# Layer 3 of a four-layer graph network: per-slot maxima on VectorE, and the destinations' scores brought to slots and edges one group earlier

## The reference

```python
h = (x @ W).reshape(N, 4, 32)
a_src = jnp.sum(h * att_src, axis=-1)        # 4 numbers a node
a_dst = jnp.sum(h * att_dst, axis=-1)
logits = leaky_relu(a_src[src] + a_dst[dst], 0.2)
seg_max = segment_max(logits, dst)
e = jnp.exp(logits - seg_max[dst])
denom = segment_sum(e, dst)
out = segment_sum(h[src] * (e / (denom[dst] + 1e-16))[:, :, None], dst)
```

## Time and profile before

| | us |
|---|---|
| median of three runs | 6190.91 |
| span of the profiled execution | 6206.6 |
| first gather of layer 3 starts | 3844.5 |
| last gather of layer 3 starts | 6151.8 |
| POOL busy, idle in that stretch | 1533.8, 786.1 |

### The profile page before, as it was taken

How to read it: one execution, slowest core, us unless ns; L and a number is a source line. 1 busy time by engine, 2 the same in 40 slices (tenths; PEclk the granted TensorE clock), 3 DMA queues, 4 the chain that set the end, 5 groups by cost and what they waited for, 6 DMA issues and landing times.

```text
span 6206.6 us, 70880 instructions
## 1 busy us (share of the span) xinstructions
PE 4537.9 (73%) x24017; PEld 3664.7 (59%) x24017; DVE 2510.7 (40%) x8563; ACT 1744.9 (28%) x3903; POOL 3119.8 (50%) x3324
## 2 busy tenths in 40 slices
PE   6999978988898988888898997254454444554445
PEld 5888865666666666666668997244343444443444
DVE  8999953333333333333335443123232222223224
ACT  5888842222222222222224553001110111101111
POOL 0000036666666666666650002666666666666664
PEclk9999989999999999999999998566566666666657
DMA  6777766655555565555556785222222222222221
GB/s 152 165 166 166 165 162 181 182 175 179 178 179 177 180 180 175 181 179 177 179 158 185 242 244 161 47 48 49 48 49 49 50 49 49 50 48 49 49 48 36
DMA packets 472459, 804.76 MB, mean 130 GB/s; under 512 B 72607, under 2 KB 301130, under 8 KB 462122
## 3 DMA queue, kind: packets, MB, share of 16 engines
q0 software_dynamic: 140192, 443.73, 28.7%
q1 hardware_dynamic: 317802, 346.76, 18.4%
q10 hardware_dynamic: 14112, 9.74, 0.5%
HBM read 663.72 MB, written 136.22 MB: 129 GB/s over the span
## 4 chain that ended last, share of the span: by engine, by line
PE 46%; another core or an unknown queue 29%; DVE 13%; issue 8%; DMA 1%; ACT 1%; POOL 0%; DVEq 0%; ACTq 0%
PE bank L1027 13%; PE bank L1014 11%; PE bank L1198 7%; PE bank L682 5%; DVE ring L1336 3%; PE bank L662 3%; DVE ring L980 2%; DMA atab<-at 1%; PE bank L1549 1%; PE bank L583 1%; DVE hs L631 1%; DVE tops L1286 1%; DVE hs L629 1%; DVE top L1290 1%
## 5 line engine op out<-in xcount | busy, mean ns | idle before, releaser
L543 POOL DMA_INDIRECT ring<-ptab,src x1612 | 1525.4, 946 | 850.4 <-issue 444.7
L543 POOL DMA_INDIRECT ring<-htab,src x1612 | 1533.8, 952 | 786.1 <-issue 465.7
L1027 PE MATMUL bank<-ring,oh 128*126 128x384 f32 x3224 | 1263.9, 508 | 32.2 <-issue 31.4
L980 DVE TENSOR_TENSOR ring<-bank,ring 128x512 f32<-128x512 f32 x806 | 543.6, 688 | 1609.3 <-PE bank L1014 737.1
L1549 PE MATMUL bank<-ring,oh 128*126 128x132 f32 x3224 | 714.5, 355 | 615.8 <-issue 605.6
L1014 PE MATMUL bank<-w1e,ea 128*128 128x256 f32 x3224 | 897.0, 401 | 244.1 <-DVE ring L980 161.1
L1549 PEld LDWEIGHTS bank<-ring,oh 128*126 128x126 f32 x3224 | 612.3, 255 | 706.9 <-issue 696.6
L1014 PEld LDWEIGHTS bank<-w1e,ea 128*128 128x128 f32 x3224 | 623.9, 200 | 528.4 <-issue 286.4
L996 ACT ACTIVATE ring<-ring 128x1024 f32<-128x1024 f32 x403 | 425.6, 1056 | 1364.8 <-DVE ring L980 1040.8
L1027 PEld LDWEIGHTS bank<-ring,oh 128*126 128x126 f32 x3224 | 625.9, 197 | 297.3 <-issue 83.5
L682 PE MATMUL bank<-xhl,at 128*126 128x258 f32 x3822 | 713.2, 323 | 0.0
(11 more groups left out here) (271 smaller groups left out, 4600.7 us busy)
## 6 DMA issues: line engine op xcount, KB each, us to landing
atab<-at POOLq DMA_DIRECT2D x78, 1543.5 KB, 9.9
ring<-ea_r SPq DMA_DIRECT2D x403, 256.0 KB
ea<-ea_t SPq DMA_DIRECT2D x403, 256.0 KB
adjb<-atab SPq DMA_DIRECT2D x156, 535.5 KB, 4.6
adjb<-atab SPq DMA_DIRECT2D x78, 472.5 KB, 4.4
ring<-ptab,src POOLq DMA_INDIRECT x1612
ring<-htab,src POOLq DMA_INDIRECT x1612
ptab<-pO ACTq DMA_DIRECT2D x49, 128.0 KB, 7.3
```

The lines of the kernel that those rows point to most:

```text
L543: return e.indirect_dma_start(o, None, table, bass.IndirectOffsetOnAxis(ap=src[:, t:t + 1], axis=0))
L980: e.tensor_tensor(group1(gi, m % 2), MLP[m % 3][:, :].rearrange("p (g f) -> p g f", g=2), group1(gi, m % 2), ALU.add).then_inc(s_edge, 1)
L1027: w = e.matmul(SUM[s % 2][0:SL, 0:384], slots_of(s, i), rv1[:, t // G % NR1, t % G, :], start=i == 0, stop=t == END[s])
```

## The change

The group's path is re-dealt. Offsets become d = u-1, a = u-2, g = u-3, c = u-4.

- **Group u**, which is just being gathered: DVE (k = 1) makes `hots` and `oh2`, k = 3 `away` (0 or -BIG, edge x slot, now from `hots` on DVE). PE (k = 4) transposes `hots` and `oh2`, both as real transposes; ACT (k = 8) copies out `ohT` and `o2T` alone. None of this needs gathered rows.
- **Group d = u-1**: PE (k = 2) brings `a_dst` to the slots into bank 5 (`s_dst`); DVE (k = 6) keeps it (`dsts`) and makes `wide4`; PE (k = 11) brings it to the edges with `ohT` (`s_ad`, half as many columns as before); ACT (k = 14) copies it into `edges`.
- **Group a = u-2**: DVE waits for the landing (before, ACT did, for u-1), adds `away` to the gathered `a_src` for each slot (`mask`, 504 columns), turns it in 32x32 squares, takes the maximum over 32, folds the four partition quarters by copies and maxima at offsets 64 and 32, spreads the result back over the quarters, picks each slot's own number with `quad` (`top`), turns the maxima back over all edges, multiplies by `hots` and adds up, so each edge has its slot's maximum without TensorE. Then logits from `edges`, `Exp` on ACT (k = 16), and the three weighings at k = 18, 19, 20.
- **Sums** of g = u-3 start at k = 0 (before, k = 4). The matmuls against `sel`, the transposing of `pk`, and the copies `pk`, `rT`, `away` on ACT are gone, `sel`'s making too. `mB` and `rB` share the memory of `held`.

```diff
-            L3A, L3B, L3G, L3C = 1, 2, 3, 4
-            LAG3 = 4
+            L3D, L3A, L3G, L3C = 1, 2, 3, 4
...
+            def before3(e, p, k):
+                if k == 1:
+                    if p >= NH:
+                        e.wait_ge(s_turn, p - NH + 1)
+                    e.tensor_tensor(hots[:, p % NH, :, :], ...
+                    if p >= ND:
+                        e.wait_ge(s_add3, p - ND + 1)
...
+                elif k == 3:
+                    e.tensor_scalar(away[:, p % NH, :, :], hots[:, p % NH, :, :], 1.0, BIG, ALU.subtract, ALU.mult).then_inc(
+            def dst3(e, d, k):
+                if k == 6:
+                    e.wait_ge(s_dst, d + 1)
+                    if d:
+                        e.wait_ge(s_ad, d)
+                    e.tensor_copy(dsts[0:SL, d % 4, :], dst_slots(d)).then_inc(s_wide, 1)
+                    e.tensor_tensor(wide4[0:SL, :, :], mine[0:SL, :].unsqueeze(2).broadcast_to([SL, GT, 4]),
...
+            def most3(e, a, k):
+                n = SIZE[a]
+                if k == 0:
+                    e.wait_ge(s_away, a + 1)
+                    e.wait_ge(*landed3(a))
+                    e.tensor_tensor(by_tile(mask, n), rows3(a, 0, n)[:, :, 128:132]...
+                elif k == 1:
+                    e.transpose(turned[:, :, :], back).then_inc(s_peak, 1)
+                elif k == 2:
+                    e.tensor_reduce(peak[:, :], turned[:, :, :], AX.X, ALU.max).then_inc(s_peak, 1)
+                elif k == 3:
+                    e.tensor_copy(other[0:64, :], peak[64:128, :]).then_inc(s_peak, 1)
+                elif k == 4:
+                    e.tensor_tensor(half[0:64, :], peak[0:64, :], other[0:64, :], ALU.max).then_inc(s_peak, 1)
...
+            def logits3(e, a, k):
+                if k == 9:
+                    e.transpose(back, peaks[:, :].unsqueeze(2).broadcast_to([P, 16, 32])).then_inc(s_pick, 1)
+                elif k == 10:
+                    e.tensor_tensor(tb, tb, each_head(hots[:, a % NH, :, :], n), ALU.mult).then_inc(s_pick, 1)
+                elif k == 11:
+                    e.tensor_reduce(zt[:, 1, 0:n, :].rearrange("p t h -> p h t"), tb, AX.X, ALU.add).then_inc(s_pick, 1)
+                elif k == 12:
+                    e.wait_ge(s_edges, a + 1)
...
             def tensor3(e):
-                        if 0 <= a < NS and k == 4:
-                            e.wait_ge(s_pack, a + 1)
-                            e.transpose(bank[4][0:4 * n, P:2 * P], pk[:, 0:n, :].rearrange("p i h -> p (i h)"), ident[:, :])
...
-                            for h in range(4):
-                                e.matmul(bank[5][0:SL, h * P:(h + 1) * P], sel[0:4 * n, h, :], rT[0:4 * n, :], start=True, stop=True)
...
+                        if u < NS and k == 4:
+                            e.wait_ge(s_hot, 2 * u + 2)
...
+                        if 0 <= d < NS and k == 2:
+                            e.wait_ge(s_copied, d + 1)
...
+                        if 0 <= d < NS and k == 11:
+                            e.wait_ge(s_wide, 2 * d + 2)
...
-                        g, i = divmod(GT * (u - L3G) + k - LAG3, GT)
+                        if 0 <= g < NS and k < SIZE[g]:
+                            if k % CH == 0:
+                                e.wait_ge(s_weigh, chunk(g, k))
```

More of the change, by code:

```diff
@@ L167, in build @@
         oh2f = oh2[:, :, :].bitcast(F32)
-        sel = sb("sel", [G * GT, 4, SL])
         mine = sb("mine", [P, GT])
@@ L1221, in expected @@
             N3 = -(-(max(POST3) + 1) // GT)
-            s_pack, s_hot, s_turn, s_away, s_copied, s_spread, s_tops, s_top, s_lim, s_wide, s_logit_in, s_logit, s_exp, s_weigh = (
-                sem(f"s_{n}") for n in ("pack", "hot", "turn", "away", "copied", "spread", "tops", "top", "lim", "wide", "logit_in",
-                                        "logit", "exp", "weigh"))
-            s_acc3 = sem("s_acc3")
+            s_hot, s_away, s_turn, s_copied, s_dst, s_wide, s_ad, s_mask, s_peak, s_top, s_lim, s_pick, s_logit, s_exp, s_weigh = (
+                sem(f"s_{n}") for n in ("hot", "away", "turn", "copied", "dst", "wide", "ad", "mask", "peak", "top", "lim",
+                                        "pick", "logit", "exp", "weigh"))
+            s_acc3, s_quad, s_edges = (sem(f"s_{n}") for n in ("acc3", "quad", "edges"))
             def odd_from(s):
@@ L1439, in vector3 @@
                 e.wait_ge(s_clear2, 1)
+                e.memset(mask[:, :, :], 0.0)
+                e.memset(quad[:, :], 0.0).then_inc(s_mask, 1)
+                e.wait_ge(s_mask, 1)
+                for k in range(4):
+                    m = e.memset(quad[32 * k:32 * k + 32, k:k + 1], 1.0)
+                m.then_inc(s_quad, 1)
+                e.wait_ge(s_quad, 1)
                 for u in range(N3):
-                    a, b, g = u - L3A, u - L3B, u - L3G
+                    d, a = u - L3D, u - L3A
@@ L1455, in scalar3 @@
                     for k in range(GT):
[L1456 to L1472 removed]
+                        if u < NS and k == 8:
+                            nb = B1[u] - B0[u] + 1
+                            e.wait_ge(s_turn, u + 1)
+                            if u >= 2:
+                                e.wait_ge(s_ad, u - 1)
+                            e.activation(ohT[0:SL, u % 2, :], bank[4][0:SL, 0:P], ACT.Copy)
+                            if u:
+                                e.wait_ge(s_dst, u)
@@ new lines, in tensor3 @@
+                        if 0 <= d < NS and k == 2:
+                            e.wait_ge(s_copied, d + 1)
+                            if d:
+                                e.wait_ge(s_wide, 2 * d)
+                            for i in range(B0[d], B1[d] + 1):
+                                m = e.matmul(dst_slots(d), o2T[:, i - B0[d], :], hs[:, i, 132:136], start=i == B0[d],
+                                             stop=i == B1[d])
+                            m.then_inc(s_dst, 1)
+                        if 0 <= d < NS and k == 11:
+                            e.wait_ge(s_wide, 2 * d + 2)
+                            if d:
+                                e.wait_ge(s_edges, d)
+                            e.matmul(bank[7][:, 0:4 * GT], ohT[0:SL, d % 2, :],
+                                     wide4[0:SL, :, :].rearrange("p t h -> p (t h)"), start=True, stop=True).then_inc(s_ad, 1)
```

274 lines of the change are left out of this document (137 added, 137 removed).

## The result

The changed kernel takes **6199.3 us** (median of 20 runs, 6192.1 to 6207.0); beside it, the kernel before took 6190.4 us (20 runs, 6183.1 to 6201.5). The ratio is 1.0016, with a 95% interval of 1.0010 to 1.0022: 9 to 10 us slower, real but within the 0.2% that I had called the same. The forecast of 6157 us was wrong. What came is rival 2's outcome, though not for rival 2's reason.

The account below looks back on a forecast made before the run. Layer 3 was taken as bound by POOL, stopped once a group by held TensorE answers. Terms -46 - 12 + 20 + 4 = -34 us took the 6206.6 us span to 6173, with the span 15.7 above the median 6157 us; range 5990 to 6330.

Parts of the forecast that it names:

- rival 2: Nothing comes of it: stop length independent of the number of answers, first stop's gain lost to longer gathers; 6180 to 6200; chance 0.17.
- the - 46 us for fewer TensorE instructions: POOL's stop in layer 3: 22 fewer TensorE instructions at 0.028 us shorten it 0.6 us a group, 77 groups.
- the + 4 us for the tail: From last gather to end, 53 us: one more DVE-heavy unit replaces one with two TensorE answers; ends 0 to +10.
- What bounds the kernel: Layer 3: POOL bound, stopped about 3.7 us a group because TensorE's answers are held while it gathers; cycle 30.0 us.
- Longer gathers (+ 20 us): POOL's gathers in layer 3: DVE's new SBUF-only operands lengthen them by 0.25 us a group.
- rival 4: DVE blocks POOL: each two-input or copying SBUF instruction holds a gather for its own length; +170 us, 6310; chance 0.08.
- The first stop (- 12 us): POOL's first stop in layer 3, 16.4 us after 105 gathers, shortens as group 0's sums need fewer answers; ends 0 and -16.
- VectorE's 4.5 us a group: DVE's net added work per group, covered by its wait for `tops`: 0 on the path, 347 us without that cover.
- Two answers in series, `dst` within the grace: TensorE's `s_dst`, then `s_ad`: `dst` by about 4 us, within some 6 us of grace; one stop a group as now.
- Rival 3: A second late TensorE answer: `dst` misses the grace, two stops a group, +285 us, 6460; in a third, 6270; chance 0.21.
- The signs that I had named: Changed profile: 78 waits of about 3.4 us, gather median 944 ns, first stop under 8 us, DVE about 13 us a group.
- The sentence on what would make the forecast wrong: Prediction wrong if DVE's own chain, not TensorE's answers, sets the unit, or held answers don't depend on POOL's gathering.

Follow-up runs that it names:

- e17: Kernel before, layer 3's gathers fetching 64 rows instead of 128, on a chip with stops: 6196.2 us, ratio 1.0011.
- e10: Kernel before with two one-column fillings on POOL behind each gather of layer 3: 6191.3 us, ratio 1.0005.
- e15: Kernel before with a 200-column filling on POOL behind each gather of layer 3, on a chip with stops: 6186.9 us, ratio 0.9998.
- e1: Changed kernel whose summing matmuls in layer 3 read only the upper 16 bits, 42 recorded instructions a group for 84: 6184.2 us, ratio 0.9992.
- e4: Changed kernel with 22 more transposes (44 recorded TensorE instructions) a group: 6209.0 us, ratio 1.0032.
- e9: Changed kernel, unchanged, run again beside the kernel before on a chip with stops: 6199.5 us, ratio 1.0020.
- e2: Kernel before with 4.5 us more VectorE work a group, six chained additions of 512 columns from SBUF: 6202.3 us, ratio 1.0023.
- e3: Changed kernel with a ring of four groups of gathered rows instead of five: 6189.7 us, ratio 0.9998.
- e11: Changed kernel with a ring of three groups of gathered rows instead of five: 6177.5 us, ratio 0.9981.
- e16: Changed kernel with a ring of three groups instead of five, second run: 6170.4 us, ratio 0.9968.
- e18: Changed kernel with a ring of three groups instead of five, third run: 6170.6 us, ratio 0.9966.
- e14: Changed kernel, unchanged, on a chip without stops: 5561.3 us against 5566.7 for the kernel before, ratio 0.9990.
- e12: Kernel before with a ring of three groups instead of five, on a chip with stops: 6509.8 us, ratio 1.0524.
- e5: Kernel before, unchanged, traced again on another chip, one without stops: 5569.0 us.
- e13: Kernel before with a 200-column filling on POOL behind each gather of layer 3, on a chip without stops: 5786.3 us against 5566.7, ratio 1.0394.

## Why the prediction was wrong, step by step

Two terms of the sum failed: the - 46 us for fewer TensorE instructions, which the runs put at 7, and the + 4 us for the tail, which measured + 22 to + 27. Under the first lies the cause that I had given to the stop.

**What bounds the kernel.** "POOL, with a stop once a group" was the right view on the wrong cause. On these chips POOL's mean pace in layer 3 is not set by its own work or by the kernel's other loads tried here. Three kernels whose POOL would by itself take 1.21 (e17), 1.26 (e10) and 1.40 us a gather (e15) had their gathers 1.421, 1.430 and 1.425 us apart. A stop has no length of its own; it is the rest, and grows with the gathers since the last one: 21 x (1.43 - 1.26) = 3.6 us, the 3.7 that I read from the earlier trace rows. "Held answers" are what this looks like from the other engines.

**The 0.028 us an instruction (- 46 us), the term that failed.** I read it from a short group: 18 tiles, stop 3.69 us instead of 3.99 and 4.06. Three tiles fewer are 12 TensorE instructions fewer, and also three gathers fewer; the second is what counts, 3 x 0.17 = 0.5 us. One row can't tell two quantities apart that always go together. e1 and e4 moved them apart and gave 0.004 us, 7 us for the 22 instructions. The gathers' stretch did get 16 us shorter (e9 against e10), so some 10 us of it have no cause that was shown.

**Longer gathers (+ 20 us).** The size was fair: 963 against 956 ns in the mean (e9, e10), 11 us. But they don't lie on the path where a stop follows; e2 had 40 us of them for nothing. The Trainium skill's lock rule ("SBUF — State Buffer", "Who interferes with whom") was weighed there as rival 4. In e2, 4.1 us of new two-input work from SBUF a group lengthened its 21 gathers by 0.53 us together. If each such instruction held POOL for its own length, it would have been some 2.7 us at POOL's share of two thirds: the trace doesn't bear the rule out in that strength.

**The first stop (- 12 us).** It is 14.51 us instead of 16.75, and comes after 119 gathers instead of 105: - 2. It is a rest too: the first gathers run at 1.25 us, and with the stop in it the mean is 1.41 us a gather in the kernel before and 1.37 us in the changed one.

**VectorE's 4.5 us a group, "off the path".** Size right (12.3 us a group, 12.9 forecast), cover right while POOL gathers, wrong once it doesn't. I had asked what the work costs without its cover and answered with 4.5 x 77 = 347 us, as if the cover went everywhere or nowhere. It goes at the end.

**The tail (+ 4 us).** It was + 22 to + 27, and this is what made the change a small loss. I counted one heavier unit. But the engines lag behind the gathers by as many groups as the ring allows, four, and after the last gather each of them costs 13 to 14 us, where the kernel before needed some 7 us. My own text had the number, POOL waits for the sums of the group five earlier; I didn't ask what that leaves to do when POOL has ended. e2 (tail + 19 with VectorE's work alone), e3 (one group less lag: 9 to 15 us less), e11, e16 and e18 (two groups less: 22 to 38 us less) and e14 (no lag: tail 5 us shorter than before) agree on it.

**Two answers in series, `dst` within the grace.** Rival 3 didn't come: 70 stops, not up to 150. The row with the long remote wait did move to `edges` (617.4 us), but ScalarE's `x2` copy (661.2) and `dsts` (556.4) have as long ones, since changes of many kinds are held alike; that no wait is special is what I missed. (The rival's two times, 6460 and 6270 us, don't follow from its price either: + 285 and + 95 us on my forecast are 6442 and 6252.)

**The signs that I had named.** Right: median gather 944, mean between 955 and 965, VectorE 12 to 13 us a group, the row of `edges`. Wrong: the first stop under 8 us, and 78 waits of 3.4 us (70, of 3.7 in the mean with the first one in it). The sentence on what would make the forecast wrong named DVE's own chain as what sets the unit; that is what happened, in the tail alone.

**The sum.** Forecast - 46 - 12 + 20 + 4 = - 34; found - 16.3 (stops, first stop and longer gathers together) and + 21.6 = + 5 in the spans of e9 and e10, + 8 to + 11 in the medians. Rival 2, "nothing comes of it", and that sentence on DVE's own chain each hold a piece: the first for the stops, the second for the tail.

## What to carry to other kernels

A wait that comes once a cycle may be a length or a rest. A trace hints at which, if it has cycles of unequal length: does the wait grow with the work since the last one? Adding work to the engine that waits tells it, and costs one run (first on the page of that run: did the work lengthen anything at all?). Where an engine's pace is set from outside, work put into its loop or taken out is worth next to nothing, and what is left is the ends: here a ring two groups shallower was worth more than the whole change, because buffers that nobody needs are work that is still to be done when the last transfer has landed. And off-path work is costed for each stretch by itself, the last units above all, times the lag with which they are reached.

## What the runs showed of the hardware

- The same program took 6188 to 6190 us on three chips and 5567 to 5569 us on two. The difference, 621 us, is in the layers with indirect gathers: 2350 against 2015 us between the first and last gather of layer 1, about 2303 against 2034 in layer 3, and some 20 us between them. Which chip one has is to be seen in one row, POOL's waits.
- On the slower chips the indirect gathers come every 1.41 to 1.43 us in the mean in layer 3 (1.459 in layer 1). That doesn't depend on POOL's own work for one (1.21 to 1.40 us) or on its rows and bytes (64 or 128 rows), and hardly on TensorE's load (337 to 781 matmuls in 300 us). While POOL would go faster than that, semaphore changes that other engines wait for are held, and VectorE's own too (1.8 us in the rows of e1). At 1.63 us (e12) none is.
- It isn't the gathers' transfers that are slow there. From the start of a gather to the end of its last DMA packet it is 2.2 us in the median in the trace of the kernel before with stops, and 2.2 us in e5 without.
- The records differ as well. Of the kernel before the packed trace holds 33,164 semaphore changes with stops and 87,956 without (e5), though both hold the same 70,880 instructions. The layers without indirect gathers have nearly all of theirs; between the first and the last gather of layer 3 it is 6,382 against 28,130, and 14,444 in e12. So "remote" often stands for a change that isn't on record. It also makes the recording itself a rival for what holds the changes back. No run here is without a trace, so that isn't shown, and what stands behind the interval stays open.
- On POOL, up to 0.15 us of filling behind an indirect gather is free: it lies in the 0.30 us of issue. A filling of 0.28 us costs 0.14 (e13).
- VectorE's turn of 32x32 squares over 128 x 512 float32 takes 0.71 us (0.69 with a broadcast operand), as long as a two-input operation on as many columns; I had taken 0.69 between bounds of 0.28 and 1.38. The groups of the changed kernel, 5100 to 5400 us:

```profile
L1380 DVE STREAM_TRANSPOSE mask<-peaks 128x512 f32<-128x512 f32 x10 | 6.9, 693 | 0.1
L1317 DVE TENSOR_TENSOR mask<-ring,away 128x504 f32<-128x504 f32 (+1 forms) x10 | 6.7, 674 | 0.0
...
L1321 DVE STREAM_TRANSPOSE turned<-mask 128x512 f32<-128x512 f32 x9 | 6.4, 711 | 0.7 <-DVE mask L1317 0.4
```
